# Attention and mixture layer: how the results of P V are turned and divided

## What is computed

```python
h = _layernorm(x) * (1 + ca) + sa
probs = softmax(einsum('bhqd,bhkd->bhqk', q, k) * hd ** -0.5)
out = einsum('bhqk,bhkd->bhqd', probs, v)
x = x + ga * (out @ proj_w.T + proj_b)
h = _layernorm(x) * (1 + cb) + sb
# the expert is the encoder/decoder pair with the least loss
x = x + gb * (h @ W_base + b_base + relu(h @ W_down[e] + bd) @ W_up[e] + bu)
```

## Time and profile before

| | |
|---|---|
| median of 3 runs | 1070.51 us (1069.71 to 1071.93) |
| profiled execution | 1072.19 us |
| its span, first to last instruction | 1070.3 us |
| granted TensorE clock, mean | 0.976 |
| PE, DVE, ACT, POOL busy | 95%, 74%, 61%, 20% |
| DMA packets | 33227, 48.58 MB |

### The profile page before, as it was taken

How to read it: one execution, slowest core, us unless ns; L and a number is a source line. 1 busy time by engine, 2 the same in 40 slices (tenths; PEclk the granted TensorE clock), 3 DMA queues, 4 the chain that set the end, 5 groups by cost and what they waited for, 6 DMA issues and landing times.

```text
span 1070.3 us, 16349 instructions
## 1 busy us (share of the span) xinstructions
PE 1012.9 (95%) x5968; PEld 509.2 (48%) x5968; DVE 795.3 (74%) x1571; ACT 651.4 (61%) x1275; POOL 210.1 (20%) x332
## 2 busy tenths in 40 slices
PE   5999999999998999999999999999999999999977
PEld 2544333434444545554444445545544554544455
DVE  3979888999887877767787877776887767695143
ACT  2138777787676665666767666555667555557610
POOL 3400141032153100003253210011461001051000
PEclk7969999999999999999999999999999999999989
DMA  6904040523304031052403204006230400110001
GB/s 163 184 1 71 2 81 11 80 59 43 65 7 70 21 46 17 6 107 73 59 11 45 37 11 60 2 12 144 49 41 2 60 1 27 60 41 2 1 1 44
DMA packets 33227, 48.58 MB, mean 45 GB/s; under 512 B 6951, under 2 KB 25388, under 8 KB 33136
## 3 DMA queue, kind: packets, MB, share of 16 engines
q1 hardware_dynamic: 32348, 46.69, 23.1%
q0 software_dynamic: 384, 0.79, 0.4%
q10 hardware_dynamic: 416, 0.08, 0.0%
HBM read 17.52 MB, written 4.22 MB: 20 GB/s over the span
## 4 chain that ended last, share of the span: by engine, by line
PE 83%; DVE 7%; ACT 6%; issue 2%; DMA 1%; SPq 0%; POOL 0%; ACTq 0%; DVEq 0%
PE pE L728 25%; PE pO L728 22%; PE pX L728 22%; PE pM L728 11%; ACT P L1033 2%; DVE mx L1162 2%; ACT h1T L1067 1%; ACT hi L1083 1%; ACT h2f L1116 1%; DVE Atok L1187 1%; DVE Hb L1317 1%; DVE lo L1250 1%; PE pX L787 1%; DVE x L1259 0%; DVE rec L1181 0%
## 5 line engine op out<-in xcount | busy, mean ns | idle before, releaser
L1162 DVE TENSOR_REDUCE mx<-pM 128x1 f32<-128x512 f32 x1006 | 630.2, 682 | 115.3 <-PE pM L728 113.0
L1033 ACT ACTIVATE P<-pE 128x512 f32<-128x512 f32 x995 | 525.6, 600 | 222.7 <-PE pE L728 219.3
L728 PE MATMUL pM<-KO,QO 48*128 48x512 f32 x1006 | 368.8, 453 | 4.7 <-DVE mx L1162 2.5
L728 PE MATMUL pE<-QO,KO 50*128 50x512 f32 x995 | 348.5, 438 | 21.5 <-DVE Atok L1187 6.7
L728 PEld LDWEIGHTS pE<-QO,KO 50*128 50x128 f32 x995 | 163.7, 187 | 232.6 <-issue 124.7
L728 PE MATMUL pO<-P,V 128*17 128x512 f32 x2048 | 257.8, 602 | 1.0 <-ACT P L1033 1.0
L728 PEld LDWEIGHTS pM<-KO,QO 48*128 48x128 f32 x1006 | 163.4, 187 | 36.1 <-DVE mx L1162 24.4
L1497 POOL CAST mh<-mxc 128x16 fp32r<-128x16 f32 x32 | 6.5, 203 | 425.2 <-DVE mxc L1171 425.1
L728 PEld LDWEIGHTS pO<-P,V 128*17 128x17 f32 x2048 | 41.5, 96 | 101.1 <-issue 95.8
L728 PE MATMUL pX<-h1T,wqkv_s 128*128 128x512 f32 x112 | 62.3, 663 | 1.2 <-DVE lo L1250 1.1
L728 PE MATMUL pX<-X,Hb 128*128 128x258 f32 x208 | 53.4, 395 | 0.2 <-ACT h1T L1067 0.2
(11 more groups left out here) (318 smaller groups left out, 981.0 us busy)
## 6 DMA issues: line engine op xcount, KB each, us to landing
KO<-hi SPq DMA_DIRECT2D x56, 128.0 KB, 4.2
QO<-hi SPq DMA_DIRECT2D x56, 128.0 KB, 5.8
x<-in_x SPq DMA_DIRECT2D x20, 256.0 KB, 3.2
out<-x SPq DMA_DIRECT2D x16, 256.0 KB, 2.2
KO<-lo SPq DMA_DIRECT2D x28, 128.0 KB, 4.0
QO<-lo SPq DMA_DIRECT2D x28, 128.0 KB, 6.2
xin<-in_x SPq DMA_DIRECT2D x12, 256.0 KB, 2.7
wd<-in_wdec SPq DMA_DIRECT2D x4, 512.0 KB, 6.0
```

The lines of the kernel that those rows point to most:

```text
L728: return e.matmul(o, lhsT, rhs, start=start, stop=stop)
L1033: e.activation(P[:, u % 3, j, :], bank(s), ACT.Exp).then_inc(*empties(s))
L1162: e.tensor_reduce(mx[:, hq % 2, k:k + 1, kh], bank(s), AX.X, ALU.max, negate=True).then_inc(*empties(s))
```

## The change

- `oturn` and `atturn` go for 31 of the 32 hq. In their place step `oput` sends, on SP's queue, for each of the four heads 16 rows of osb to their place in AT (a buffer of its own now) and the row of sums to 32 partitions of `orow`, 16 numbers on each: eight transfers.
- `orec`: VectorE takes the reciprocal of `orow` (128x16), and one transfer brings it to `sums` in DRAM.
- `oget`: four transfers read each head's 512 reciprocals from DRAM to 16 partitions of `asum`.
- `onorm`: POOL multiplies AT by asum where it stands, for two hq at a time (one in one case), 128x512 or 64x512.
- The last hq keeps `oturn` and one `atturn`.
- ScalarE's copy to osb waits for all twelve transfers of `oput` and `oget` of the hq before, where it waited for `oturn`.
- `wpg` and `wbg` are loaded from DRAM anew for every block and gated in place; `wp_s`, `wb_s` and `Atok` are gone. `enc` no longer waits for `proj`.
- In `order()`, where no long step is ready behind a burst, a PV step is put there.

```diff
@@ -69,9 +69,6 @@
...
             for u, ks in halves:
-                for th in sorted({k // 2 for k in ks}):
-                    if q == LAST or th == 1:
-                        at(u - 4, ("atturn", q, th), ("atturn", q, 2 + th))
                 for k in ks:
...
@@ -90,10 +87,8 @@
...
         if b < NB:
-            if b < LAST:
-                at(B + 55, ("atturn", b, 0), ("atturn", b, 2))
             u = B + (20 if b == LAST else 53)
-            at(u, ("prep", b))
+            at(u, ("prep", b), ("wbload", b))
             for k in range(4):
...
@@ -112,8 +107,14 @@
...
         return [(("mmax", b), 1.2)]
-    if kind == "oturn":
+    if kind == "oput":
         return [(("gates", 8), 0), (("PV", 8 * b + 7), 0.6)]
+    if kind == "orec":
+        return [(("oput", b), 1)]
+    if kind == "oget":
+        return [(("orec", b), 1)]
+    if kind == "onorm":
+        return [(("oget", hq), 1.5) for hq in parts(*s[1:])]
     if kind == "wload":
...
         return [(("mid", b - 1, 0), 1)] if b else []
+    if kind == "wbload":
+        return [(("xsq", b - 1, 1), 0)] if b else []
     if kind == "prepb":
-        return [(("prep", b), 1)] + ([(("out", b - 1, 3), 1)] if b else [])
+        return [(("prep", b), 1), (("wbload", b), 2)] + ([(("out", b - 1, 3), 1)] if b else [])
     if kind == "xload":
...
     if kind == "proj":
-        return [(("atturn", b, a[0] // 2 + i), 0) for i in (0, 2)] + [(("addx", b, a[0]), 1)]
+        return [(("onorm", b, i, a[0] // 2), 0.7) for i in range(2)] + [(("addx", b, a[0]), 1)]
     if kind == "bn2":
...
@@ -180,9 +180,11 @@
...
-def turned(b, k):
-    return max(SEQ.index((4 * b + 2 * (k // 2) + i, k % 2)) for i in range(2))
+def parts(b, cc, half):
+    hqs = [SEQ.index((4 * b + 2 * cc + i, half)) for i in range(2)]
+    return [hq for hq in hqs if hq < NU // 8 - 1]
...
@@ -322,7 +324,11 @@
...
         if w % 8 == 7 and w < NU - 1:
-            waiting["short"].append(("oturn", w // 8))
+            hq = w // 8
+            b, g = divmod(SEQ[hq][0], 4)
+            waiting["quiet"][:0] = [("oput", hq), ("orec", hq), ("oget", hq)]
+            if hq == parts(b, g // 2, SEQ[hq][1])[-1]:
+                waiting["quiet"].insert(3, ("onorm", b, g // 2, SEQ[hq][1]))
...
@@ -368,7 +374,12 @@
...
         else:
+            stood = len(out)
             credit, filled = long(u, min(credit + SHARE[min(int(u) // UB, LAST)], 2 if light else 3.5), 2 - light)
+            if len(out) == stood and some:
+                weigh(pv, u)
+                pv += 1
         for _ in range(2 - (filled > 1)):
...
@@ -511,7 +523,9 @@
...
         osb = sb("osb", [128, 512])
-        Atok = sb("Atok", [128, 8, D])
+        AT = sb("AT", [128, 2, T])
+        asum = sb("asum", [128, 2, 512])
+        orow = sb("orow", [128, 16])
         xin = sb("xin", [128, 2, D])
...
@@ -522,9 +536,7 @@
...
         wqkv_s = sb("wqkv_s", [128, 2, 3 * D])
-        wp_s = sb("wp_s", [128, 2, D])
         wpg = sb("wpg", [128, 2, D])
-        wb_s = sb("wb_s", [128, 2, D])
         wbh = sb("wbh", [128, 2, D], R)
...
@@ -662,9 +680,10 @@
...
-        def rows_of(b):
-            return h1T if b == LAST else AT
+        def stored(hq):
+            c = SEQ[hq][1]
+            return d_put[c], 16 * 8 * sum(x[1] == c for x in SEQ[:hq + 1])
...
@@ -846,34 +865,33 @@
...
                 elif kind == "atturn":
-                    b, k = s[1:]
-                    c, th = k // 2, k % 2
-                    pe.wait_ge(*emptied("oturn", turned(b, k)))
+                    pe.wait_ge(*emptied("oturn", NU // 8 - 1))
                     for t in range(4):
-                        a = e.transpose(o[:, 128 * t:128 * t + 128],
-                                        Atok[:, 4 * th + t, 128 * c:128 * c + 128], ident)
+                        a = e.transpose(o[:, 128 * t:128 * t + 128], Alast[:, t, :], ident)
                     a.then_inc(*fills(s))
...
                     pe.wait_ge(*vacant(p))
-                    pe.wait_ge(*emptied("atturn", b, k // 2))
+                    pe.wait_ge(s_at, nth["onorm", b, 0, k // 2])
                     pe.wait_ge(s_wpg, b + 1)
...
                         tt = 2 * k + t
-                        mm(bank(p)[:, 256 * t:256 * t + 256], rows_of(b)[:, 0, 128 * tt:128 * tt + 128], wpg[:, 0, :],
+                        mm(bank(p)[:, 256 * t:256 * t + 256], AT[:, 0, 128 * tt:128 * tt + 128], wpg[:, 0, :],
                            t == 0, False)
...
                     t = piece
-                    for i in (0, 2):
-                        pe.wait_ge(*emptied("atturn", b, k // 2 + i))
+                    for i in range(2):
+                        pe.wait_ge(s_at, nth["onorm", b, i, k // 2])
+                    if begun(s):
+                        pe.wait_ge(*emptied("atturn", b, 3))
                     pe.wait_ge(s_wpg, b + 1)
...
                         tt = 2 * k + t
-                        a = mm(o[:, 256 * t:256 * t + 256], rows_of(b)[:, c, 128 * tt:128 * tt + 128], wpg[:, c, :],
+                        a = mm(o[:, 256 * t:256 * t + 256], AT[:, c, 128 * tt:128 * tt + 128], wpg[:, c, :],
                                c == 0, c == 1 and (t == 1 or not begun(s)))
...
@@ -1035,7 +1053,7 @@
...
                     if hq:
-                        act.wait_ge(*full("oturn", hq - 1))
+                        act.wait_ge(*stored(hq - 1))
                     act.wait_ge(s_pv, s[1] + 1)
...
@@ -1093,15 +1111,9 @@
...
                 elif kind == "atturn":
-                    b, k = s[1:]
-                    c, th = k // 2, k % 2
-                    if b < LAST:
-                        act.wait_ge(*(full("gram", b - 1, 3) if b else full("setupc")))
-                    else:
-                        act.wait_ge(*full("qk", b, 3, 1))
-                        act.wait_ge(*full("v", b, 3))
+                    act.wait_ge(*full("proj", LAST - 1, 3))
                     act.wait_ge(*full(*s))
-                    e.activation(rows_of(b)[:, c, 512 * th:512 * th + 512], bank(s), ACT.Copy).then_inc(*empties(s))
+                    e.activation(AT[64:128, 1, 512:1024], bank(s)[64:128, :], ACT.Copy).then_inc(*empties(s))
...
@@ -1170,19 +1182,17 @@
...
+                elif kind == "orec":
+                    hq = s[1]
+                    dve.wait_ge(d_orow, 64 * (hq + 1))
+                    e.reciprocal(orow[:, :], orow[:, :]).then_inc(s_rsum, 1)
                 elif kind == "oturn":
-                    hq = s[1]
-                    gi, c = SEQ[hq]
-                    b, g = divmod(gi, 4)
                     v = bank(s).rearrange("p (k j e) -> p k j e", k=4, j=4)
-                    if hq:
-                        dve.wait_ge(*emptied("oturn", hq - 1))
                     dve.wait_ge(*full(*s))
                     e.reciprocal(rec[:, :, :], v[:, :, :, HD]).then_inc(*link.up())
-                    dst = Atok[:, 4 * c:4 * c + 4, 64 * g:64 * g + 64].rearrange("p k (j e) -> p k j e", j=4)
-                    if b:
-                        dve.wait_ge(*full("atturn", b - 1, 3))
-                    dve.wait_ge(s_gates, 1)
+                    dst = Alast[:, :, 64:128].rearrange("p k (j e) -> p k j e", j=4)
+                    dve.wait_ge(*full("ln1turn", LAST, 3))
                     dve.wait_ge(*link.now())
...
@@ -1309,8 +1319,8 @@
...
                     dve.wait_ge(s_nbe, 1)
-                    if b < LAST:
-                        dve.wait_ge(*full("proj", b, 3))
+                    dve.wait_ge(*full("setupc"))
+                    dve.wait_ge(*full("modmm", 2))
                     if b:
...
@@ -1507,23 +1517,28 @@
...
                     pool.wait_ge(d_bc, 64 * (b + 1))
-                    pool.wait_ge(d_w[4], 16)
-                    if b:
-                        pool.wait_ge(*full("proj", b - 1, 3))
-                    e.tensor_tensor(wpg[:, :, :], wp_s[:, :, :], bc[:, 0:1, :].to_broadcast([128, 2, D]),
+                    pool.wait_ge(d_wp, 16 * (b + 1))
+                    e.tensor_tensor(wpg[:, :, :], wpg[:, :, :], bc[:, 0:1, :].to_broadcast([128, 2, D]),
                                     ALU.mult).then_inc(s_wpg, 1)
...
+                elif kind == "onorm":
+                    b, cc, half = s[1:]
+                    p1 = 64 * len(parts(b, cc, half))
+                    rows = AT[0:p1, cc, 512 * half:512 * half + 512]
+                    for hq in parts(b, cc, half):
+                        pool.wait_ge(*stored(hq))
+                    e.tensor_tensor(rows, rows, asum[0:p1, half, :], ALU.mult).then_inc(s_at, 1)
                 elif kind == "prepb":
                     b = s[1]
-                    pool.wait_ge(d_w[5], 16)
+                    pool.wait_ge(d_wb, 16 * (b + 1))
                     pool.wait_ge(d_bc, 64 * (b + 1))
...
                         pool.wait_ge(*full("out", b - 1, 3))
-                    pool.wait_ge(s_xsq, 4 * b)
-                    e.tensor_tensor(wbg, wb_s[:, :, :], bc[:, 3:4, :].to_broadcast([128, 2, D]),
```

(45 more changed lines are left out.)

11 lines of the change are left out of this document (5 added, 6 removed).

## The result

The changed kernel takes 1083.66 us (median of 4 runs, 1082.27 to 1085.57) against 1071.22 us for the kernel before on the same chip (4 runs, 1069.71 to 1073.27). The ratio is 1.0116, 95% interval 1.009 to 1.0142: 12.4 us slower, where 13 us less was forecast and 1071 was the upper end of the range.

The account below looks back on a forecast made before the run. PE (TensorE) was taken as the bound nearly everywhere, DVE close behind in some bursts. 1072.2 - 22.1 + 7 + 1.5 + 0.5 = 1059.1 us profiled, 1057.4 on the median; range 1043 to 1071.

Parts of the forecast that it names:

- Theory 1: Experiments' theory: turns worth about the forecast; DVE's orow waits, from SP's earlier work, eat it; clock lengthens each stop.
- The turns, 22.1 us: On PE, 46 groups of four transposes go at 0.48 us each: 22.1 us less, ends 3 and 34.
- The wait that comes, 7 us: DVE's reciprocal waits for rows of sums at eight places, 11 us; PE loses 7 us, ends 0 and 29.
- The other edits, nothing: PV steps put forward, enc free of proj, AT its own buffer: work on PE only moved, cost nothing.
- SP's queue, 1.5 us: 403 added transfers delay the maxima queued behind them and oget: 1.5 us more, 0 to 10.
- POOL and proj, 0.5 us: 16 POOL products, 20 us on an engine 20% busy; first half's proj waits: 0.5 us more, 0 to 4.
- PE busy near 987 us: Sign expected in the profile after: PE's busy time falls to near 987 us from 1013.
- Rival 3: Reciprocal waits everywhere because transfers of sums land slowly: 1079 us; sign, over 30 us of DVE's waits; chance 0.10.
- Rival 2: SP's serial queue sets the pace, E steps wait for maxima, over 5 us in all: 1066 us; chance 0.16.
- Rival 1: Each group of turns gives full 0.59 us and DVE catches up behind every wait: 1044 us; chance 0.15.
- Rival 4: Turns were nearly free on PE, 0.06 us a group, gain 3 us, waits still paid: 1076 us; chance 0.05.
- the 0.7 us worked out from it: Skill's 2.0 us counted from the end of the 0.6 us issue: every landing 0.7 us later, estimate 1063.

Follow-up runs that it names:

- run 4: Changed kernel without its 403 transfers, reciprocals, ScalarE's wait for them and POOL's products, nothing in the turns' place: 1043.42 us, ratio 0.9701 to the kernel before.
- run 10: Changed kernel without the transfers, DVE's 31 reciprocals and POOL's products for blocks 1 to 3 kept on constants: 1045.71 us, ratio 0.9715 to the kernel before.
- runs 11: Changed kernel without reciprocals and POOL's products, all 13 transfers of each hq going into tiles no engine reads: 1062.06 us, ratio 0.9873 to the kernel before.
- run 12: Changed kernel without reciprocals and POOL's products, transfers into unread tiles, x loaded from ScalarE's queue instead of SP's: 1044.97 us, ratio 0.9708 to the kernel before.
- run 2: Changed kernel with DVE's reciprocal taken of a constant tile, so it waits for no transfer; all transfers still go: 1062.83 us, ratio 0.9909 to the kernel before.
- run 1: Changed kernel with oput, orec and oget of hq 8 placed later in the list, behind proj(0, 3): 1075.68 us, ratio 1.0025 to the kernel before.
- run 9: Kernel before with 20 needless DVE operations ahead of the reciprocal at hq 8, 12, 16 and 20: 1115.83 us, ratio 1.038 to the unaltered one.
- run 7: Changed kernel with hq 8's transfers behind proj(0, 3), rows of sums sent first, every reciprocal one unit later: 1056.59 us, ratio 0.9843 to the kernel before.

## Why the prediction was wrong, step by step

The account, at 1071.2: 32 us gained by the turns' going and the edits beside it (run 4); 1.5 given back by reciprocals and products (run 10); 18.4 by transfers that hold the loads of x (runs 11, 12); 22 by the reciprocals' waits (run 2), of which 9.8 is the one hold at hq 8 (run 1). 1071.2 - 32 + 1.5 + 18.4 + 22 = 1081.1 against 1083.7 measured; the 2.6 left are within the intervals, which leave each of these terms 4 to 7 us of room. Theory 1 held, but with a part that it lacked, the loads of x.

- **The turns, 22.1 us.** Right in sign, too small: 32, or 0.70 a group, close to the upper end of 0.74, if all of it is the turns'. The products by themselves are worth 0.31, below the 0.48 taken; the rest comes from what hangs on them or from the other edits, which isn't shown. The view of one burst against another priced products only.
- **The wait that comes, 7 us.** This step failed: 22 us and not 7. With the one on SP's queue it turned the sign. What failed is the count: 11 us of DVE at 8 places, in fact 34.9 at 13. The queue was reckoned as free wherever no copies stood; it was held by `fetch` at hq 21 and by `proj` at hq 8, and one place at rest, with 2.5 us to spare, stood for 23, where hq 30 waited 1.4 us with the queue free. The landing was right in the median (1.8 us for 1.9), but 3.8 at hq 4 and 25. The price of a microsecond of wait came out as forecast, 22 for 34.9 where it was 7 for 11, and that is luck. The banks took up more than the 0.6 us a wait that I gave them (PE waited 21.3 us in all for reduces), and the clock, for which the sum has no term, gave it back: PE stood 2.64 us of the 6.1 at hq 25 and then ran at 0.52 for 6 us. A long stop costs more than its length, 10.2 for 9.2 (run 9).
- **The other edits, nothing.** This failed, and cost most for one line: 9.8 of the 22 us above (run 1). "AT as its own buffer" brings SP a wait for the projection of the block before, and I did not compare its place in the list with that of hq 8.
- **SP's queue, 1.5 us.** The mechanism was right and the victim wrong: I looked at the maxima, which nobody waits for, and not at the other loads of the same queue. 18 us and not 1.5, outside the ends of 0 to 10. That the new wait of the copy to osb would cost nothing was right: ScalarE never waits for these transfers there.
- **POOL and proj, 0.5 us.** Right within error (run 10: 1.5). POOL's 50.5 us of waits for asum held nobody long: PE waited 0.2 us for AT.
- **PE busy near 987 us.** It is 1015.1. The turns have gone, but products at 1.2 GHz take longer, 0.79 us for one of pM behind the stop at hq 8 and 0.46 in the mean of all 1006; where no reciprocal waits and x comes in time (run 12) it is 995.1.
- **Rivals.** Rival 3 had the sign and nearly the time (1079), by the wrong mechanism: landing is not slow. Its mark, over 30 us of DVE's waits, was met by another cause, which is why a mark should name what sets it. Rival 2 (SP sets the pace, 1066) had the queue right and what waits behind it wrong: its mark, E steps that wait for the maxima, isn't there, and the price was too small. Rival 1's 1044 is near what runs 4 and 12 reach with the waits away. Rival 4 fell (run 4). The Trainium skill's fixed 2.0 us ("DMA: Bandwidth & Descriptors", anatomy of one DMA) is given there for transfers that GpSimd issues. On SP's queue the 2 KB transfers landed 1.8 us after their issue began and the 8 KB to DRAM 1.4 us after, so neither the 0.7 us worked out from it nor a longer way to DRAM is seen here.

What stays open: how much of the gain beyond the products is whose, and how the 15 us between the best version (1054.4) and run 4 divide. It has the loads of x on SP's queue still, but in its trace DVE waits only 0.5 us for them; some 5 us of it lie behind the last copy to osb, where 57.4 us are left and run 4 has 52.3.

## What to carry to other kernels

A transfer is priced by what stands before and behind it on its queue: its own landing was right to 0.1 us here in the median, and the 13 transfers of each hq lost 40 us by what they waited for and what waited for them, of which 29 came back by moving steps alone (run 7). For every wait that an edit adds, look up in the list whether what it waits for stands ahead of the first step that hangs on it; if not, the engine stops there, and all that hangs on its later steps with it. Charge a stop of the bound engine at more than its length: here its clock was down for the next 6 us or more once it had stood for 2.6 us.
